# Attention with 8 batches of 4 head groups: x for the next batch loaded turned and normalised by GpSimd, stacks filled through DRAM, projections reordered

## The reference, cut to what matters

```python
# x, ctx: (8, 512, 512); 16 heads of 32
xn = layernorm(x)
Q = xn @ q_w.T + q_b;  K = ctx @ k_w.T + k_b;  V = ctx @ v_w.T + v_b
scores = where(mask, -1e9, Q @ K.T / sqrt(32))      # per head
x = x + tanh(g_xattn) * (softmax(scores) @ V @ o_w.T + o_b)
xn = layernorm(x)
xr, xk = mu_r * xn + (1 - mu_r) * prev(xn), mu_k * xn + (1 - mu_k) * prev(xn)
x = x + tanh(g_ffn) * sigmoid(xr @ W_r.T) * (relu(xk @ W_k.T) ** 2 @ W_v.T)
```

## Time and profile before

| | |
|---|---|
| three runs | 1232.02, 1234.52, 1234.85 us |
| the profiled execution | 1232.68 us, span 1230.8 us |
| granted clock, mean | 0.99 |
| PE, DVE, ACT, POOL busy | 95%, 77%, 61%, 19% |
| DMA, mean | 90 GB/s, queues 31% |

### The profile page before, as it was taken

The page is one execution under the profiler, slowest core; times in us unless marked ns, Lnnn a source line. Parts: engine busy times, 40 slices in busy tenths (PEclk is TensorE's granted clock), DMA queues, the critical chain, the costliest instruction groups (busy, mean ns, idle before and its releaser), DMA issues.

```text
span 1230.8 us, 22178 instructions
## 1 busy us (share of the span) xinstructions
PE 1167.7 (95%) x7424; PEld 921.5 (75%) x7424; DVE 942.5 (77%) x2011; ACT 745.2 (61%) x1619; POOL 237.4 (19%) x427
## 2 busy tenths in 40 slices
PE   3999999999999999999999999977999999999997
PEld 2777776777777777777677777754888888888886
DVE  5778788788878887878878887879677677777763
ACT  4578778678768877877867876764432333233232
POOL 2030030030021003003003000024423433332431
PEclk9999999999999999999999999987999999999999
DMA  6433342253243333344225322452111311311200
GB/s 218 120 94 83 101 122 66 63 157 81 71 129 89 81 102 100 82 104 118 67 60 159 78 74 65 123 168 76 59 52 60 95 52 52 104 52 52 97 25 35
DMA packets 72703, 110.33 MB, mean 90 GB/s; under 512 B 14864, under 2 KB 23696, under 8 KB 72592
## 3 DMA queue, kind: packets, MB, share of 16 engines
q1 hardware_dynamic: 72592, 108.92, 31.1%
HBM read 41.76 MB, written 16.78 MB: 48 GB/s over the span
## 4 chain that ended last, share of the span: by engine, by line
PE 76%; DVE 9%; issue 6%; ACT 4%; DMA 4%; SPq 1%; POOL 0%; POOLq 0%; ACTq 0%; DVEq 0%
PE bank L445 24%; PE bank L509 14%; PE bank L476 12%; PE bank L521 10%; PE bank L502 7%; PE bank L485 6%; DMA x_rows<-x 3%; DVE neg_s L857 3%; ACT probs L681 2%; PE bank L491 2%; PE bank L575 1%; DVE pT L863 1%; DVE xh L973 1%; DMA pT<-wkT 1%; DVE ctx_sb L848 1%
## 5 line engine op out<-in xcount | busy, mean ns | idle before, releaser
L681 ACT ACTIVATE probs<-neg_s,negmax 128x512 f32<-128x512 f32 x512 | 367.9, 720 | 40.5 <-DVE negmax L857 39.4
L857 DVE CUSTOM_DVE_ANT_0 neg_s<-bank,mask_big 128x512 f32<-128x512 f32 x512 | 344.7, 683 | 19.2 <-PE bank L502 16.9
L509 PE MATMUL bank<-ident,probs 128*128 128x128 f32 x2048 | 314.8, 276 | 17.3 <-ACT probs L681 16.8
L509 PEld LDWEIGHTS bank<-ident,probs 128*128 128x128 f32 x2048 | 240.4, 141 | 75.6 <-ACT probs L681 40.7
L863 DVE COPY pT<-bank 128x512 f32<-128x512 f32 x256 | 176.5, 690 | 120.8 <-PE bank L509 119.7
L502 PE MATMUL bank<-k_stack,q_stack 96*128 96x512 f32 x512 | 243.3, 475 | 6.0 <-DVE negmax L857 5.9
L688 ACT COPY pT<-bank 128x512 f32<-128x512 f32 x256 | 149.4, 584 | 98.3 <-PE bank L509 92.5
L1068 POOL TENSOR_SCALAR var_eps<-mv 128x2 f32<-128x2 f32 (+1 forms) x24 | 18.5, 770 | 639.9 <-DVE mv L822 578.3
L521 PE MATMUL bank<-pT,v_sb 128*32 128x512 f32 x1024 | 118.5, 603 | 0.8 <-issue 0.5
L779 ACT ACTIVATE relu<-bank 128x512 f32<-128x512 f32 x32 | 19.2, 598 | 149.0 <-PE bank L445 149.0
L502 PEld LDWEIGHTS bank<-k_stack,q_stack 96*128 96x128 f32 x512 | 97.3, 190 | 11.2 <-DVE negmax L857 8.5
(11 more groups left out here) (110 smaller groups left out, 2125.1 us busy)
## 6 DMA issues: line engine op xcount, KB each, us to landing
k_stack<-k_hi SPq DMA_DIRECT2D x256, 64.0 KB, 2.0
q_stack<-q_hi SPq DMA_DIRECT2D x256, 64.0 KB, 2.0
x_rows<-x SPq DMA_DIRECT2D x8, 1024.0 KB, 6.6
cT_raw<-ctxT SPq DMA_DIRECT2D x8, 1024.0 KB, 5.8
k_stack<-k_lo SPq DMA_DIRECT2D x128, 64.0 KB, 2.0
q_stack<-q_lo SPq DMA_DIRECT2D x128, 64.0 KB, 2.0
ctx_dram<-ctx_sb SPq DMA_DIRECT2D x32, 256.0 KB, 2.1
c_raw<-ctx_dram SPq DMA_DIRECT2D x16, 512.0 KB, 5.1
```

The source lines that it names most:

```text
L509: mm = nc.tensor.transpose(pt_bank[i % 2][:, a * P:(a + 1) * P], probs[:, i % P_RING, a * P:(a + 1) * P], ident[:])
L681: nc.scalar.activation(probs[:, i % P_RING, :], neg_s[:, i % SM_RING, :], ACT.Exp, bias=negmax[:, k:k + 1], scale=-1.0, accum_out=den[:, g ...
L857: nc.vector.tensor_tensor_reduce(neg_s[:, i % SM_RING, :], s_bank[i % S_BANKS][:], mask_big[:, q, :], 1.0, 3e38, ALU.add, ALU.min, negmax[ ...
```

## The change

For batches 1 to 7 x now comes in twice. ACT's queue loads four slices of 128 rows (`load_rows`), on which DVE takes the statistics; GpSimd makes mean and 1/std (`rstd_of`), ACT stores them to DRAM (4 KB) and loads them back spread to all partitions (`spread_mean_rstd`, 512 KB). ACT also loads x already turned (`xT_d`, a new input that the host turns) in four slices of 256 KB (`load_xT`). GpSimd subtracts the mean row (`centre`), multiplies (`scale_rows`), ACT rounds (`x_rounded`), GpSimd takes the rest (`x_rest`); so also `c_rest` for ctx. The `T` and `C` items of batches 0 to 6 are gone; the prologue keeps its own for batch 0. The stacks are filled by store and load: `q_hi`, `q_lo`, `k_hi`, `k_lo` go whole to `qk_dram` (256 KB each), and six DMAs of 32 partitions x 4 heads (256 KB) bring them back. PE waits for the whole stack before the first head. `K n` is in steps 0 to 4 of every group, each group has one K, one V and one Q; `V 1` is made in group 0 of its own batch, `V 2` and `V 3` one group later than before. `store_context` comes behind `stack_group` on SP.

```diff
 PE_SIDE = [
+    parts("K", 1, 0, 1, 3, 4) | parts("V", 1, 5, 6, 7, 8, 9, 10) | parts("Q", 2, 12, 13, 14, 16),
+    parts("K", 2, 0, 1, 3, 4) | parts("Q", 3, 6, 7, 8, 9) | parts("V", 2, 10, 11, 12, 13, 14, 15),
+    parts("K", 3, 0, 1, 3, 4) | parts("V", 3, 5, 6, 7, 8, 9, 10) | parts("Q", 4, 12, 13, 14, 16),
+    parts("K", 4, 0, 1, 3, 4) | parts("V", 0, 6, 7, 8, 9, 10, 11) | parts("Q", 5, 12, 13, 14, 16),
 ]
-STATS_STEPS = (8, 10, 12, 14)
+def prepare_at(nb):
...
+    return {(first, 3, 0): ("rows", 0), (first, 3, 2): ("rows", 1), (first, 3, 4): ("xT", 0), (first, 3, 6): ("xT", 1),
+            (first, 3, 10): ("rows", 2), (first, 3, 12): ("rows", 3), (then, 0, 12): ("store", 0),
+            (then, 0, 14): ("spread", 0), (then, 1, 10): ("hi", 0), (then, 1, 12): ("hi", 1), (then, 1, 14): ("xT", 2),
+            (then, 2, 0): ("xT", 3), (then, 2, 4): ("hi", 2), (then, 2, 6): ("hi", 3)}
+def stats_at(nb):
+    return ((0, 0, 5), (0, 0, 7), (0, 0, 13), (0, 0, 15)) if nb == 1 else (
+        (nb - 2, 3, 7), (nb - 2, 3, 9), (nb - 1, 0, 3), (nb - 1, 0, 5))
+def c_hi_at(nb):
+    return tuple((nb - 1, 2, i) for i in (11, 12, 13, 14))
-PROLOGUE = C_ITEMS + [("K", 0)] + T_ITEMS + [("Q", 0), ("V", 0), ("V", 1), ("Q", 1)]
+PROLOGUE = C_ITEMS + [("K", 0)] + T_ITEMS + [("Q", 0), ("V", 0), ("Q", 1)]
...
+            def store_part(g, which, part):
+                source = (qk_hi, qk_lo)[part][which]
+                sp.dma_start(qk_dram[g, which, part], source[:].bitcast(F32)).then_inc(part_st[which][part], 16)
+            def load_bands(g, which, part):
+                sp.wait_ge(part_st[which][part], (g + 1) * 16)
+                for band in range(BANDS):
+                    if ((0, 0, 1), (0, 1, 0))[which][band] == part:
+                        sp.dma_start(stack[g % 2][which][HD * band:HD * (band + 1), :, :].bitcast(F32),
+                                     qk_dram[g, which, part].rearrange("(j d) t -> d j t", j=GH)).then_inc(stacked[which], 16)
             def stack_group(b, n):
+                store_q(b, n)
+                sp.wait_ge(s_mm, (g - 1) * TILES + HEAD)
+                load_bands(g, 0, 0)
+                load_bands(g, 0, 1)
+                store_k(b, n)
+                load_bands(g, 1, 0)
+                load_bands(g, 1, 1)
...
+            def centre(b, a):
+                pool.wait_ge(xT_ld[a % 2], ((b - 1) * 2 + a // 2 + 1) * 16)
+                pool.wait_ge(mr_ld, b * 16)
+                nc.gpsimd.tensor_tensor(x_rows[:, 2 + a % 2, :], x_rows[:, 2 + a % 2, :], x_rows[:, 0, :],
+                                        ALU.subtract).then_inc(x_mid, 1)
+            for b in range(1, B):
+                rstd_of(b)
+                for pair in ((0, 1), (2, 3)):
+                    for a in pair:
+                        centre(b, a)
+                    for a in pair:
+                        scale_rows(b, a)
+                    for a in pair:
+                        x_rest(b, a)
+                for a in range(CH):
+                    c_rest(b, a)
```

More of the change, by code:

```diff
@@ L261, in hi_no @@
                 return [i for i in PROLOGUE if i[0] != "V"].index(item)
-            order = [i for i in (ORDER_LAST if isinstance(b, int) and b == B - 1 else ORDER) if i[0] != "V"]
+            order = [i for i in (ORDER_LAST if b == B - 1 else ORDER) if i[0] != "V"]
             return b * HI_PER_BATCH + HI_PROLOGUE + order.index(item)
@@ L411, in batch @@
                 store_context(b, GROUPS - 1)
-            for b in range(B - 1):
+            for b in range(B):
                 batch(b)
-            batch(B - 1)
             for s in range(2):
@@ new lines, in c_rounded, with prepare @@
+            def c_rounded(nb, a):
+                act.wait_ge(side_mm, mm_no(nb - 1, ("V", 3)) + 1)
+                act.wait_ge(c_ld, nb * 16 + 16)
+                nc.scalar.copy(act_hi[1][:, a, :], cT_raw[:, a, :]).then_inc(ct_hi, 1)
+            def prepare(b, c, i):
+                for nb in (b + 1, b + 2):
+                    if nb < B and (b, c, i) in prepare_at(nb):
+                        what, n = prepare_at(nb)[b, c, i]
+                        if what == "rows":
+                            load_rows(nb, n)
+                        if what == "xT":
+                            load_xT(nb, n)
+                        if what == "store":
+                            store_mean_rstd(nb)
+                        if what == "spread":
+                            spread_mean_rstd(nb)
+                        if what == "hi":
+                            x_rounded(nb, n)
+                    if nb == b + 1 < B and (b, c, i) in c_hi_at(nb):
+                        c_rounded(nb, c_hi_at(nb).index((b, c, i)))
@@ L712, in tile_step @@
                     probs_out(b, c, i)
[L714 to L719 removed]
             def batch(b):
                 for c in range(GROUPS):
[L723 removed]
+                    for i in range(TILES):
                         tile_step(b, c, i)
+                        if b and (c, i) == (0, HI_STEP):
+                            side(b - 1, "R", GROUPS - 1)
+                        prepare(b, c, i)
                         if is_last(b) and (c, i) in SPLIT_W2:
@@ L974, in normalise2 @@
                                             ALU.subtract, ALU.mult).then_inc(xh_done, 1)
-            early_steps(0)
-            for b in range(B - 1):
+            for b in range(B):
                 batch(b)
-            batch(B - 1)
             def difference(b, h):
@@ L1161 @@
     ctx_dram = nc.dram_tensor("ctx_dram", (B * D, S), F32, kind="Internal").ap()
-    build(nc, *args, out, ctx_dram)
+    qk_dram = nc.dram_tensor("qk_dram", (B * GROUPS, 2, 2, P, S), F32, kind="Internal").ap()
+    mr_dram = nc.dram_tensor("mr_dram", (B, 2 * S), F32, kind="Internal").ap()
+    build(nc, *args, out, ctx_dram, qk_dram, mr_dram)
     result = run_bass_kernel_spmd(nc, [arrays], core_ids=[0])
```

252 lines of the change are left out of this document (132 added, 120 removed).

## The result

The changed kernel takes 1253.18 us, the median of 4 runs (1251.75 to 1254.83), beside 1233.42 for the kernel before (4 runs, 1232.02 to 1234.85). The ratio is 1.016, 95% interval 1.0143 to 1.0177: it is slower, where 1207 was forecast. The profiled execution took 1251.75, its span 1250.0, 19.2 us more than the span in the earlier trace rows.

What follows compares the result with a forecast made beforehand. PE, and what keeps it waiting, was taken to set the time. Gains of 21.0 us (batches 1 to 6), 1.7 (batch 0 and prologue) and 2.5 (last group) sum to 25.2: 1232.7 to 1207.5, stated as 1207, range 1191 to 1229.

Steps and rivals of the forecast that it cites:

- Stacks, "the price is nothing": Step 14: path from k_lo through DRAM to the loaded stack takes 6.5 us, within 8.2 us available, so no cost.
- the stack comes late: Rival, chance 0.12: last band lands over 8.2 us after k_lo, PE waits 1.4 us in 31 groups: 1251.
- Waits in front of ACT's issues, "should be met": ACT's queue: 4 KB store lands within two steps, some 2.6 us, so ACT does not wait before its issues.
- The start, "a loss of 1.0": Prologue: first stack through DRAM, up to 2 us later first scores, partly offset; a net loss of 1.0 us.
- Order of the items, evening out: Stage 1 groups: one K, V and Q each makes all four cost 23.54 us, saving 5.90 us a batch.
- DMA issues on ACT, 0.8 a batch: ACT's ten DMA issues a batch cost a quarter of 10 x 0.33 us, 0.8 us given back.
- Statistics, 1.0: Groups 3 and 0: statistics of x and aggregates stay, so about 1.0 us a batch is given back.
- ACT's copies, 0.6 a batch: Groups 1 and 2: ACT's x and ctx copies give back 0.1 and 0.5 us a batch.
- Batch 7's groups 0 to 2, "will again": Batch 7: groups 0 to 2 took 70.60 us and will take the same again.
- Last group, -2.5: Batch 7's last group: GpSimd's x_in addition finishes earlier and no longer delays c_lo, saving 2.5 us.
- GpSimd, 1.2 us an operation: GpSimd's 16 operations of 128x512 a batch take 1.2 us each, 19.5 us in all, hidden.
- GpSimd and DVE block each other: Rival, chance 0.08: GpSimd holds DVE's copy of the reciprocals, 3 us a batch, 19 in all: 1226.

Runs made afterwards that it cites:

- the sixth run: Changed kernel with the stacks filled as before, by 24 DMAs of 64 KB from SBUF per group, all else as changed: 1226.70 us, ratio 0.9964.
- the third run: Changed kernel with a batch's last context store issued behind the next batch's first stacks, and the 1 MB ctx load one group later: 1223.30 us, ratio 0.992.
- the base: The kernel of the third run, on which later edits were tried: changed kernel with context store behind and ctx load late, 1223.30 us.
- the fifth: Changed kernel with one edit only, the next batch's 1 MB ctx load issued in group 1 instead of group 0: 1241.56 us, ratio 1.008.
- the second: Changed kernel with the context store of a batch's last group issued behind the stacks of the next batch's group 1: 1245.33 us, ratio 1.0098.
- the first run: Changed kernel with the spread load of mean and 1/std moved from step 14 of group 0 into group 1: 1246.23 us, ratio 1.0106.

## Why the prediction was wrong

- *Stacks, "the price is nothing".* This is the step that failed. The path from `k_lo` was 10.4 us in group 0 of batch 3, not 6.5: the store landed after 5.0 us, where issue and landing had 2.4, and the last load after 5.0 and not 3.5. I took landings from a queue in which transfers followed each other 0.61 us apart, and asked only how large they are. What I left out is what else the new order puts beside them: q loads in front, 1 MB right behind, and SP's queue held by the context's store. The rival *the stack comes late* had the mechanism and, by chance, 1251; but it was priced at 1.4 us in 31 groups. It came at 1.5 to 3.4 us in group 0 of each batch, 4.5 in the first, and next to nowhere else. The clock that falls behind the wait was in neither: 1.7 us a batch by the estimate above. By the page "DMA: Bandwidth & Descriptors" of the Trainium skill (Anatomy of one DMA) the load would have taken an estimated 2.6 us, and the trace has 4.1 at the median. The page gives that figure for one DMA that GpSimd issues; these were issued by SP, three together.
- *Waits in front of ACT's issues, "should be met".* Wrong in group 0. The 4 KB landed after 5.9 us, not 2.1 to 2.6. The same page warns that the write receipt can be long where the target is HBM, and I had weighed that warning for the stacks alone. The runs do not show that the target is the reason: the same store lands after 1.9 us in the sixth run, and after over 5 only where 1 MB of ctx stands right before it. Both waits together, with the low clock behind them: 102.36 us a batch with them, 97.97 without them, 4.4 us a batch and 26 us for six, of the 30 that the third run won.
- *The start, "a loss of 1.0".* It lost 7.85 up to the first context; the rest of batch 0 gained 1.6, where 2.8 was forecast. The first stack through DRAM and the clock after it account for most of it: 6.3 go with the old stacks (69.47 against 63.19; 3.6 at the end of batch 0), 3.5 of the base's with the first stack alone.
- *Order of the items, evening out.* Right for group 3, which fell from 26.33 to 23.6 to 24.2 us, where I had 24.3.
- *DMA issues on ACT, 0.8 a batch.* Too high. An issue lies beside a running exponential, changed kernel, ACT's timeline:

```profile
342.32 0.72 ACT L761 ACTIVATE probs<-neg_s,negmax 128x512 f32<-128x512 f32 x1
342.38 0.33 ACTq L706 DMA_DIRECT2D x_rows<-x  x1
```

  Group 3 has six of them and is the shortest group. What costs is a wait in front of an issue. That the issues themselves cost nothing is read from this; no run took them away.
- *Statistics, 1.0.* A little low. Without the DMA waits, groups 0 and 3 take 24.8 and 23.9 us on average in the third run, 1.6 over 47.08. If the issues cost nothing, this is what the statistics and the aggregates cost; with the issues' 0.8 the forecast had 1.8 for the two groups, so its sum was right there.
- *ACT's copies, 0.6 a batch.* Mis-sized, 2.2: group 1 takes 24.39 (0.85 over 23.54, 0.1 was taken), group 2 takes 24.9 (1.35 over, 0.5 was taken). These 1.6 us too little make up the whole distance from 96.56, forecast, to 97.97. But the copies are not the whole cause: in group 1 0.62 of the 0.85 stands in batch 7 as well, where no x is copied; most likely it belongs to the order of the items, whose gain the forecast took in full. For group 2 the cause stays open.
- *Batch 7's groups 0 to 2, "will again".* Put at nothing, and 2.6 us longer (73.20 for 70.60): group 0 waits 1.46 us for its stack, group 1 takes 24.16 and group 2 23.29.
- *Last group, -2.5.* Right in sign and about in size, -3.15 in this trace (the runs above have -1 to -4), for the reason given. GpSimd's addition to `x_in` now ends before DVE's `c_lo` begins, timelines of the changed kernel:

```profile
828.28 2.37 POOL L1185 TENSOR_TENSOR x_in<-x_in,tgbo 128x1024 f32<-128x1024 f32 x1 [95.06 <-DMA x_in<-x]
...
836.98 1.23 DVE L1013 TENSOR_TENSOR c_lo<-c_raw,c_hi 128x1024 fp32r<-128x1024 f32 x1 [1.07 <-ACT c_hi L823]
...
838.95 1.62 PE L471 MATMUL bank<-w2o_lo,c_hi 128*128 128x512 f32 x4 [2.48 <-DVE ctx_sb L922]
```

  `c_lo` takes 1.23 us for 3.22, PE waits 2.48 for 4.47.
- *GpSimd, 1.2 us an operation.* Right, 1.28 to 1.29. The rival *GpSimd and DVE block each other* came true in its mechanism: the copy of the reciprocals takes 1.35 to 1.41 us in group 2 of batches 1 to 7 of the changed kernel, and 0.43 in the other groups of batches 1 to 6, as in all of them before. It ends beside the context matmuls, and in the third run no wait of PE above 0.7 us follows it, so no price of it shows.

In sum, the measured 19.2 us lie 44.4 from the forecast's -25.2: 26.4 are the two waits and the clock behind them in batches 1 to 6, 8.4 the rest of these batches, groups 1 and 2 above all, 8.0 batch 0 and what comes ahead of it, 2.6 batch 7's groups 0 to 2, less 1.0 in the last group and after it. With its two waits taken away the change is worth 10 us, not 25.

## What to carry to other kernels

When many small transfers become few large ones, the queue moves up: work out for each transfer what is in flight beside it in the new order, not how long its like took in the old one. Put a large load that nobody needs soon behind the small transfers on which an in-order engine waits, and a store that must wait for its data behind those whose data is ready. Look at the first group of a batch and at the start on their own, since a price that is nothing in three groups of four can still decide the time. And read the granted clock behind a wait of PE: here the wait was paid a second time in it.

## What was not expected of the hardware

- The same store of 4 KB to DRAM lands after 1.9 us at the median in the sixth run, 2.7 in the third, 3.7 in the fifth, 5.4 in the second, 5.9 in the changed kernel and 6.3 in the first. The last three are the kernels in which 1 MB of ctx is issued right before it. The fifth run has none there and 3.7 all the same, so the load is not the whole of it. The context's store of 256 KB lands after 4.6 us at the median right behind the three k loads, where it took 2.1 ahead of the stacks and takes 2.3 in the sixth run, with the old stacks.
- Loads of 256 KB into 32 partitions land after 3.8 to 4.1 us (page, third run and changed kernel), where stores of 256 KB out of 128 partitions land after 2.1 to 2.7 (`k_hi`, `k_lo`). The loads also come three together, so the shape alone is not shown to be the cause.
- Two waits on two engines hid each other: removed one at a time they gave 8 and 12 us, together 30.
- A wait of PE of 2.2 to 3.4 us in group 0 was followed by 3.4 us at a granted clock of 0.50 in five batches of the changed kernel; behind 1.46 us in its batch 7, and behind 2.54 us in batch 3 of the first run, the clock stayed at 1.00.
